# GpSimd's indirect calls: waiting for the call ahead before every call, or before every second one

## The reference, cut to what matters

```python
x = x + 0.5 * _L0_ffn_ref(_layernorm(x), ...)
x = x + _L0_attn_ref(_layernorm(x), ...)
x = x + 0.5 * _L0_ffn_ref(_layernorm(x), ...)
x = x + 0.5 * _L1_ffn_ref(_layernorm(x), ...)
x = x + _L1_attn_ref(_layernorm(x), ...)
x = x + 0.5 * _L1_ffn_ref(_layernorm(x), ...)
...
topk_w, topk_idx = jax.lax.top_k(logits, K)          # K = 2 of E = 8 experts
h = jax.nn.silu(g) * u
out = jnp.einsum('ted,te->td', y, combine)
```

## Time and profile before

| | |
|---|---|
| median of 3 runs | 792.03 us (790.85 to 794.85) |
| the profiled execution | 796.77 us |
| its span, first to last instruction | 794.9 us |
| PE busy | 620.6 us, 78% of the span |
| POOL busy | 388.9 us, 49% |
| DVE busy | 388.5 us, 49% |
| ACT busy | 343.6 us, 43% |
| mean granted TensorE clock | 0.900 |

### The profile page before, as it was taken

How to read it: one execution, slowest core, us unless ns; L and a number is a source line. 1 busy time by engine, 2 the same in 40 slices (tenths; PEclk the granted TensorE clock), 3 DMA queues, 4 the chain that set the end, 5 groups by cost and what they waited for, 6 DMA issues and landing times.

```text
span 794.9 us, 13288 instructions
## 1 busy us (share of the span) xinstructions
PE 620.6 (78%) x4180; PEld 523.5 (66%) x4180; DVE 388.5 (49%) x1056; ACT 343.6 (43%) x667; POOL 388.9 (49%) x400
## 2 busy tenths in 40 slices
PE   2489759988697977869789859689778889977780
PEld 2389657678566967768678758357644558876770
DVE  6543116876868744532224034667777855400102
ACT  2346437734366534536544435213222224645340
POOL 1545655664465545555545555622204454455552
PEclk9989988999699999989988989989869989989795
DMA  9541113111311213221321131100301001212213
GB/s 340 185 172 38 31 44 84 37 35 58 84 34 33 65 31 94 64 38 44 90 62 40 37 90 38 33 17 14 88 9 28 17 27 34 61 40 75 66 41 109
DMA packets 45122, 50.22 MB, mean 63 GB/s; under 512 B 14456, under 2 KB 36344, under 8 KB 45056
## 3 DMA queue, kind: packets, MB, share of 16 engines
q0 software_dynamic: 11776, 24.14, 12.2%
q1 hardware_dynamic: 33280, 25.23, 10.0%
HBM read 32.04 MB, written 17.29 MB: 62 GB/s over the span
## 4 chain that ended last, share of the span: by engine, by line
PE 37%; DMA 25%; issue 20%; POOL 8%; DVE 7%; ACT 3%; POOLq 0%; ACTq 0%; DVEq 0%; SPq 0%
DMA xs<-tokens_in,idx_in 15%; PE bank L615 10%; DMA tokens_out<-ys,idx_out 9%; PE bank L595 9%; PE bank L602 4%; POOL xs L1088 4%; PE pair L735 3%; POOL tokens_out L1100 3%; PE pair L703 2%; PE pair L539 2%; PE bank L576 2%; PE pair L519 1%; PE pair L529 1%; ACT ys L902 1%; DVE x L1283 1%
## 5 line engine op out<-in xcount | busy, mean ns | idle before, releaser
L1100 POOL DMA_INDIRECT tokens_out<-ys,idx_out x184 | 192.2, 1044 | 193.5 <-ACT ys L902 77.9
L1088 POOL DMA_INDIRECT xs<-tokens_in,idx_in x184 | 186.8, 1015 | 189.5 <-issue 59.3
L615 PE MATMUL bank<-w,hT 128*128 x1288 | 187.7, 292 | 12.0 <-ACT ys L902 3.2
L615 PEld LDWEIGHTS bank<-w,hT 128*128 128x128 f32 x1288 | 172.0, 205 | 29.4 <-issue 28.2
L595 PE MATMUL bank<-xT_kept,w_up 128*128 128x128 f32 x1104 | 160.9, 293 | 13.1 <-issue 5.2
L595 PEld LDWEIGHTS bank<-xT_kept,w_up 128*128 128x128 f32 x1104 | 146.8, 206 | 27.5 <-issue 17.1
L834 ACT ACTIVATE w_up<-w 128x728 f32 (+1 forms) x184 | 128.8, 717 | 41.2 <-DVE owner L1247 19.4
L576 PE MATMUL bank<-const,xs 128*128 128x128 f32 x184 | 42.1, 304 | 89.5 <-DMA xs<-tokens_in,idx_in 88.5
L1267 DVE TENSOR_TENSOR hT<-gate,bank 128x384 f32<-128x384 f32 x92 | 50.7, 551 | 124.2 <-PE bank L595 57.2
L1283 DVE SCALAR_TENSOR_TENSOR x<-yg,cw,x 128x128 f32<-128x128 f32 x128 | 37.5, 340 | 146.4 <-DMA yg<-tokens_out 146.2
L602 PE MATMUL bank<-xT_kept,w_up 128*128 128x128 f32 x736 | 106.2, 294 | 0.2
(11 more groups left out here) (169 smaller groups left out, 629.6 us busy)
## 6 DMA issues: line engine op xcount, KB each, us to landing
yg<-tokens_out SPq DMA_DIRECT2D x64, 128.0 KB
w<-in_w SPq DMA_DIRECT2D x8, 536.0 KB, 8.2
w<-in_w SPq DMA_DIRECT2D x8, 512.0 KB
xs<-tokens_in,idx_in POOLq DMA_INDIRECT x184
tokens_out<-ys,idx_out POOLq DMA_INDIRECT x184
tokens_in<-xn SPq DMA_DIRECT2D x8, 256.0 KB
tokens_in<-xn SPq DMA_DIRECT2D x8, 254.0 KB
out<-x SPq DMA_DIRECT2D x8, 128.0 KB
```

Of the source, the lines that this page charges most:

```text
L615: last = mm(y, hT[0:n_f, n % 2, c * P:(c + 1) * P], w_of(k, e, WD[k] + c * P, P, n_f), start=(c == 0), stop=(k == 0 and c == CH[k] - 1))
L1088: pool.indirect_dma_start(xs[:, j % RING, :], None, xn_dram[KIND[f]][b], tile_rows(idx_in, b, j), engine_sem=described)\
L1100: pool.indirect_dma_start(ys_dram[b], tile_rows(idx_out, b, j), ys[:, j % RING, :], None, engine_sem=described)\
```

## The change

A counter over all indirect calls, gathers and scatters together in POOL's order, starts at 0. The wait on `described` is put only before the calls with an even number (but the first); it still asks for all the calls before. A call with an odd number follows the call ahead with no wait on it. All waits on data are as they were.

```diff
@@ -42,6 +42,7 @@
 RING = 8
+BURST = 2
@@ -1066,10 +1067,10 @@
             calls = itertools.count()
 
-            def one_at_a_time():
+            def pair_done():
 
                 n = next(calls)
-                if n:
+                if n and n % BURST == 0:
                     pool.wait_ge(described, n)
@@ -1084,7 +1085,7 @@
-                    one_at_a_time()
+                    pair_done()
                     pool.indirect_dma_start(xs[:, j % RING, :], None, xn_dram[KIND[f]][b], tile_rows(idx_in, b, j),
```

## The result

The changed kernel takes **733.16 us** (732.14 to 734.59, 4 runs) where the kernel before takes 793.44 (790.85 to 796.61, 4 runs). The ratio is 0.924 with an interval of 0.9198 to 0.9282, so 60.3 us less. The forecast was 766 and the range 744 to 806: the direction was right, and more than half of the gain was missed. The profiled execution took 734.59 us with a span of 732.7 and a mean granted TensorE clock of 0.922 (before 794.9 and 0.900).

A forecast was written before the change was run, and what follows sets the result against it. POOL's handing over between indirect calls was taken to set the pace where POOL leads, with PE next. 71 x 0.74 x 0.5 = 26 us off the median 792.0 gave 766 us, range 744 to 806.

The forecast's parts named there:

- rival with a slower kernel: Odd calls directly behind even ones are drawn out, to 2.0 or 2.12 us start to start: 796 to 824 us, chance 0.25.
- Only those on the chain count: Of 184 odd calls losing their wait, only the 83 on the profile's written chain of waits save time.
- the twelve that I struck out beside the first mixer: Twelve of the 83, at 140 to 180 and 200 to 245 us beside vector work, counted as nothing, leaving 71.
- Let PE give up half: Of the time freed on POOL, half reaches the end: 12.4 us in the four stretches, the same half elsewhere.
- the four stretches: Where POOL leads the chain longest: 144 us, PE idle 24.9, 32 of the 83 waits, worth 23.7 us.
- 0.02 us left of the gap: Ahead of an odd call on POOL, 0.02 us of gap stays without its wait, so 0.74 us less each.
- other end (0.46): The other bound for an odd call's saving: 0.30 us of its gap stays, 0.46 us goes.
- the row of a cast behind a scatter: A POOL cast with waits long met starts 0.01 us after a scatter; taken as nearest to an unwaited odd call.
- The clock: The granted clock, 0.84 to 0.96 in the four stretches, may rise a little with shorter PE pauses; counted as nothing.
- if PE follows fully, 731 us: Larger gain: all 83 x 0.74 = 61 us arrive, 731 us; the case 731 to 750 had chance 0.07.
- The estimate by the Trainium skill: From dispatch and semaphore times, a removed wait frees 0.15 us, 83 of them 12 us; the time falls by 6 us.
- the smaller gain: 0.30 us of each gap ahead of odd calls stays, 16 us go: 776 us; case 776 to 787, chance 0.13.

The follow-up runs named there:

- e2: The kernel before without the wait on the call ahead before the 101 odd calls not on its written chain: 773.06 us, ratio 0.9704.
- e14: The kernel before without the wait before the 101 odd calls off its written chain, repeated on another chip: 761.72 us, ratio 0.9579.
- e15: The kernel before with no call waiting for the end of another, the waits for data kept: 681.33 us, ratio 0.8549.
- e6: The changed kernel with true waits before every fourth call only, and already met waits on `described` before the calls halfway between: 701.33 us, ratio 0.8819.
- e11: The kernel before with all waits on the call ahead kept but moved behind the data's wait, on a third chip: 684.14 us, ratio 0.8604.
- e16: The kernel before with all waits on the call ahead kept but moved behind the data's wait, on a fourth chip: 681.80 us, ratio 0.8569.

## Why the prediction was wrong

**The mechanism was right.** The removed waits were part of POOL's beat, PE follows when they go, and calls are not drawn out. Calls take 1.04 us on the mean after against 1.03 before, and no rival with a slower kernel came near: start to start an odd call needs 1.27 us, far from the 1.73 at which that rival decided. Four steps of the sum were off, three low and one high.

**"Only those on the chain count"** is the step that failed most. It took 83 of 184 calls, although 161 had a gap to lose. e2 and e14 removed only calls that this step priced at nothing, and they gave 23.0 us and, on an undisturbed chip, 33.8. The written chain names one path at each moment. Where POOL's beat and PE's work run side by side it may be written through PE, while POOL still sets how fast tiles arrive. Calls 147 to 177 show that: POOL is never idle there for more than 0.81 us, twelve of the fifteen odd calls are off the chain, and e14, which removed those twelve waits alone, takes 46.81 us for the stretch instead of 52.56. That is 5.75 us less, against 12 x 0.45 = 5.4. The same holds for the twelve that I struck out beside the first mixer: the second of those two stretches (200 to 245 us) became 7.8 us shorter, the first 2.1.

**"Let PE give up half"** was a choice with no row behind it. Half was set against 0.74 us a call; against the true 0.45 the four stretches gave 91%, and the whole kernel 83%. Of PE's idle time there, 26.3 us, the change took 10.9, not far from the 12.4 that I expected; but the rest was no way through copy and activation, for in e15, with no wait at all, only 2.6 us of it are left. And 5.5 us came from PE's own work at the higher clock, for which the sum had no term. The text also calls 12.4 us half of the 23.7; it is half of the 24.9.

**"0.02 us left of the gap"** was wrong in the other direction. 0.30 stays (e15), so a call was worth 0.45, which the text had as its other end (0.46). I chose by the row of a cast behind a scatter, but a cast is not an indirect call: the calls of the earlier trace rows that follow after 0.30 us were the nearer rows. The text had read them rightly as far as the 0.45 goes, as the time to take up a call after a wait ahead of it, and then assumed that the rest hung on the semaphore. It does not. (That every call in the trace has at least 0.30 us ahead of it holds between two calls only: the scatter at 86.12 starts 0.16 us after a vector instruction of POOL.)

**The clock**, for which I counted nothing, rose from 0.900 to 0.922, and PE's work shrank by 13.0 us, a fifth of the gain.

With the measured terms the sum reads 161 x 0.45 x 0.83 = 60 us, but the 0.83 is itself the measured gain over 161 x 0.45, so this closes by construction; with the 0.91 of the four stretches it would read 66. With the gap of 0.45 and my own other two steps it would have been 71 x 0.45 x 0.5 = 16, so that the forecast was 26 and not 16 is luck: a gap taken too large made up for a part of what the other steps lost. The figure "if PE follows fully, 731 us" came closest, by 83 x 0.74 = 61 us for the wrong reason. The range was cut at 744, too tight for a sum with two factors of choice in it.

**The estimate by the Trainium skill**, "DMA: Bandwidth & Descriptors", "Anatomy of one DMA" (0.15 us a wait, 6 us in all) was low by three times for each wait: 0.45 us was measured.

**What the signs said.** Odd calls within 0.05 us: no, 0.30. Even calls keep 0.75: yes. A pair takes 2.7 us: no, 3.00. PE's wait for gathered rows at 50 to 70: 49.4. PE over 80% busy: 83%. A gap of 0.30 had been named as the sign of the smaller gain; it came with the larger one.

## What to carry to other kernels

A wait's price can lie in its place and not in what it waits for: where an instruction has two waits, let it hold the one that ends last, and put the one that is long met ahead of it. Here that edit alone, with every wait kept, gives 682 to 684 us on two chips, 50 us less than dropping half of the waits, but 825 on a third, so it should be timed on more than one. This was seen on POOL's indirect calls alone. When a beat repeats for hundreds of microseconds, price each of its gaps over all repetitions by the time between equal calls, and not by the share that the written chain happens to show. Look in such a stretch for waits that the change can't explain before putting the difference down to it.

## What the runs showed of the hardware that was not expected

- In none of the 18 profiles here do two indirect calls of POOL follow each other in less than 0.30 us, with or without a wait; a wait that is an instruction of its own and ends last makes it 0.75. A wait ahead that has long been met costs nothing (0.30 us in e6). After ACT's copy a call starts in 0.28 us where it holds the wait, and in 0.75 us where the wait stands ahead of it (e11).
- On one chip, two kernels with mostly 0.30 us gaps took 824.8 and 791.4 us instead of 684.1 and 701.9 elsewhere, repeatably in 4 and 8 runs, with 68 us and 54 us of the span put down to "another core or an unknown queue" and waits of up to 10.4 us on ACT and DVE at once. The kernel before took 796.0 us there, as elsewhere; its only profile, from a chip that is not on record, has four such waits of up to 8.7 us. They do not always end with a burst of calls: in the place shown, DVE goes on in the midst of one. What is held up (instructions, semaphores or something at the memory), and why so much more on that chip, was not found; that chip was not used again, so a passing condition of that chip is not excluded either.
- The granted TensorE clock was higher in the kernels in which PE stood idle less: 0.900 with 174 us of idle time before, 0.922 with 125 us after, 0.953 with 96 and 95 us in e11 and e16.
